# A two-layer transformer kernel: the second attention in row and column parts, five tiles in turns

## The reference

```python
h = _layernorm(x) * (1 + ca) + sa
q = (h @ Wq + bq).reshape(B, S, 16, 32);  kv = (h @ Wkv + bkv).reshape(B, S, 2, 4, 32)   # 4 kv heads
q = apply_rope(q, pos);  k = apply_rope(kv[:, :, 0], pos)
for qs in range(0, S, 128):                       # chunks of 128 queries
    ls = max(16, qs - 127)
    k_c = concat(k[:16], k[ls:qs + 128])           # 16 meta keys, this chunk, the chunk before
    scores = q_c @ k_c.T / sqrt(32)                # masked: causal, and within 128 or meta
    y_c = softmax(scores) @ v_c
x = x + ga * (y @ Wo + bo)
```

## Time and profile before

| | us |
|---|---|
| median of 3 runs | 2404.34 (2399.58 to 2405.88) |
| the profiled execution | 2407.0 |
| its span, first to last instruction | 2405.2 |
| PE busy | 2165.4 (90%) |
| PEld busy | 1492.4 (62%) |
| DVE busy | 1123.3 (47%) |
| ACT busy | 766.4 (32%) |
| POOL busy | 779.6 (32%) |

### The profile page before, as it was taken

How to read it: one execution, slowest core, us unless ns; L and a number is a source line. 1 busy time by engine, 2 the same in 40 slices (tenths; PEclk the granted TensorE clock), 3 DMA queues, 4 the chain that set the end, 5 groups by cost and what they waited for, 6 DMA issues and landing times. The chain is left out here.

```text
span 2405.2 us, 41150 instructions
## 1 busy us (share of the span) xinstructions
PE 2165.4 (90%) x11700; PEld 1492.4 (62%) x11702; DVE 1123.3 (47%) x2783; ACT 766.4 (32%) x1814; POOL 779.6 (32%) x1344
## 2 busy tenths in 40 slices
PE   4799877999999999999916999999994999999998
PEld 2676544555555555555504777777782887878787
DVE  2467575565552222222235676666543454343432
ACT  0233244222222222222202555444552332322322
POOL 0243302223333333333268766677312201101000
PEclk7899888999999999999957999999997999999999
DMA  7555542665565566656443222222001212222220
GB/s 243 183 203 199 218 125 84 195 201 176 183 203 183 191 214 203 203 189 221 136 150 89 72 56 57 72 71 72 2 1 53 70 62 79 62 73 67 72 68 27
DMA packets 122498, 302.21 MB, mean 126 GB/s; under 512 B 24864, under 2 KB 28576, under 8 KB 122272
## 3 DMA queue, kind: packets, MB, share of 16 engines
q1 hardware_dynamic: 73376, 179.04, 22.3%
q0 software_dynamic: 23040, 75.52, 11.1%
q10 hardware_dynamic: 25984, 46.38, 5.2%
HBM read 216.47 MB, written 83.36 MB: 125 GB/s over the span
## 5 line engine op out<-in xcount | busy, mean ns | idle before, releaser
L1167 PE MATMUL bank<-arena 128*128 x1272 | 446.4, 494 | 10.7 <-issue 9.2
L1167 PEld LDWEIGHTS bank<-arena 128*128 128x128 f32 x1272 | 229.8, 191 | 148.5 <-issue 17.9
L1184 PE MATMUL bank<-arena 96*128 x632 | 297.5, 593 | 0.0
L1288 DVE TENSOR_TENSOR arena<-bank,mod 128x512 f32<-128x512 f32 x158 | 109.3, 692 | 214.8 <-PE bank L1184 178.1
L1890 PE MATMUL bank<-x_hi,w_hi 128*128 128x512 f32 x512 | 200.8, 392 | 6.0 <-DVE x_lo L2023 6.0
L1890 PE MATMUL bank<-x_hi,w_lo 128*128 128x512 f32 x512 | 199.4, 389 | 0.0
L1890 PE MATMUL bank<-x_lo,w_hi 128*128 128x512 f32 x512 | 199.2, 389 | 0.0
L1283 DVE TENSOR_TENSOR arena<-arena,bank 128x192 f32<-128x192 f32 x159 | 56.3, 354 | 303.5 <-ACT arena L1205 303.1
L1200 ACT COPY arena<-bank 96x256 f32<-96x256 f32 x158 | 58.2, 368 | 423.2 <-issue 221.2
L1704 DVE TENSOR_REDUCE arena<-bank 128x1 f32<-128x272 f32 x256 | 112.1, 438 | 169.3 <-PE bank L1589 157.8
L1146 POOL DMA_INDIRECT arena<-h_moe,arena x160 | 158.5, 991 | 75.7 <-issue 73.0
(11 more groups left out here) (331 smaller groups left out, 4293.5 us busy)
## 6 DMA issues: line engine op xcount, KB each, us to landing
arena<-in_moe_up SPq DMA_DIRECT2D x64, 768.0 KB, 7.1
y_moe<-arena ACTq DMA_DIRECT2D x158, 256.0 KB, 2.7
y_moe<-mod SPq DMA_DIRECT2D x32, 1024.0 KB
ffn_arena<-in_ffn_up SPq DMA_DIRECT2D x64, 512.0 KB, 3.5
arena<-in_moe_down SPq DMA_DIRECT2D x64, 384.0 KB, 9.4
arena<-in_L_wmod SPq DMA_DIRECT2D x12, 1024.0 KB, 7.0
x_res<-in_L_attn_x SPq DMA_DIRECT2D x1, 4096.0 KB
h_moe<-arena SPq DMA_DIRECT2D x16, 256.0 KB, 6.7
```

The source lines that it names most:

```text
L1167: mm = nc.tensor.matmul(psum[2 + b][:, 0:2 * FI], xgT[:, b, k], up_ring[:, bass.ds((e % RING) * UPW + k * 2 * FI, 2 * FI)], start=(k == 0) ...
L1184: mm = nc.tensor.matmul(psum[6 + b][:], hiddenT[:, b, n], down_ring[:, bass.ds((e % RING) * DOWNW + n * C, C)], start=(n == 0), stop=(n == 1))
L1288: nc.vector.tensor_tensor(y[:, b], psum[6 + b][:], mod[:, 0, 5], ALU.mult).then_inc(y_out, 1)
```

## The change

`schedule` now unrolls 22 turns (m = -4 to 17). A turn works on up to seven tiles: `g` = m+4 (gather), `y` = m+3 (add the experts, statistics), `p` = m+2, `f` = m+1, `s` = m (scores, maxima, exponentials), `a` = m-1 (transposes of the probabilities, values), `w` = m-2 (division, output projection). Heads are handled four at a time (`c` = 0 to 3).

- Scores: four matmuls, each with the 32 rows of one head, into banks 0 to 3. `kT` has no zeros. The mask matmul is gone.
- VectorE adds the mask, negates and takes the minimum in one pass of 272 columns per head (L1690), which writes the negated masked scores to SBUF; a subtraction prepares the meta columns of four heads (L1694).
- ScalarE takes the exponentials in SBUF, 256 columns per head, and once per tile those of all meta columns.
- The probabilities are transposed one tile later, eight transposes for four heads into banks 4 and 5, and copied 512 columns at a time.
- Values: `v` (32 columns) is stationary and 512 columns of transposed probabilities of four heads stream; head group `c` writes partitions 32c to 32c+31 of bank 4. The same with a matrix of ones into bank 5 gives the sums. The meta keys are added by 16 matmuls of 128 columns into each. The result is already transposed: L1647 and L1750 have nothing that answers to them.
- The division is a reciprocal of 128x512 sums and a multiply of 128x512, at the start of VectorE's next turn.
- GpSimd gathers in groups of 3, 2 and 3 (before: eight in a row), the first tile's ahead of its memsets, and reads the positions directly. The values' copies to `v` are gone: VectorE writes them into a ring of five tiles.
- Several buffers lie in `mod[:, 0]` and `down_scale`; `wo` is loaded in four pieces.

```diff
-                    turn(*[tile(t + n) for n in stages])
+                for m in range(-4, NT + 2):
+                    turn(g=tile(m + 4), y=tile(m + 3), p=tile(m + 2), f=tile(m + 1), s=tile(m), a=tile(m - 1), w=tile(m - 2))
...
-                            nc.tensor.matmul(bank, ident_b[:], mask1[:, kind], start=True, stop=False)
-                            nc.tensor.matmul(bank, qT[:, b, n // HP], kT[:, n // HP, n % HP], start=False, stop=True).then_inc(s_mm, 1)
+                def scores(t, c):
+                    if c == 0:
+                        pe.wait_ge(q_in, t + 1)
+                        pe.wait_ge(k_in, t + 1)
+                    pe.wait_ge(mx_done, NHEAD * t + HP * c)
+                    for r in range(HP):
+                        q = slice(HD * r, HD * r + HD)
+                        nc.tensor.matmul(psum[r][:, 0:KEYS1], qT[q, t % 2, c], kT[q, c], start=True, stop=True).then_inc(s_mm, 1)
...
-                            nc.tensor.matmul(out, probT[:, one % 4, 0:P], v[:, 0, c], start=False, stop=False)
+                def turn_probs(t, c):
+                    pe.wait_ge(exp_done, NHEAD * t + HP * c + HP)
+                    if c == 0 and t:
+                        pe.wait_ge(o_out, t)
+                    pe.wait_ge(pT_out, copies_before(t, c))
+                    for k in chunks(t):
+                        for r in range(HP):
+                            at = META + P * k
+                            mm = nc.tensor.transpose(psum[4 + k][:, r * P:(r + 1) * P], slot(t, c)[:, r, at:at + P], ident[:])
...
+                        pe.wait_ge(pT_out, copies_before(a + 1, 0))
+                        pe.wait_ge(pM_out, a + 1)
+                        for bank, local, meta in ((b_o, lambda k, c: v[:, keys_of(a, k) % VRING, c], lambda r, c: v_meta[:, c // 2, r, c % 2]),
+                                                  (b_sum, lambda k, c: ones_f, lambda r, c: meta_sum[:, r, c % 2])):
+                            for k in chunks(a):
+                                for c in range(NKV1):
+                                    nc.tensor.matmul(bank[HD * c:HD * c + HD], local(k, c), probT[:, k, c].rearrange("p r n -> p (r n)"),
+                                                     start=(k == 0), stop=False)
+                            for r in range(HP):
+                                for c in range(NKV1):
+                                    mm = nc.tensor.matmul(bank[HD * c:HD * c + HD, r * P:(r + 1) * P], meta(r, c), metaT[:, c // 2],
+                                                          start=False, stop=(r == HP - 1))
+                                    if r == HP - 1:
+                                        mm.then_inc(o_mm, 1)
...
-                            nc.vector.tensor_reduce(nmx[:, b, n:n + 1], psum[n % 4][:, 0:KEYS1], AX.X, ALU.max,
-                                                    negate=True).then_inc(mx_done, 1)
+                        nc.vector.tensor_tensor_reduce(slot(t, c)[:, r], psum[r][:, 0:KEYS1], mask1[:, kind], -1.0, 3e38, ALU.add, ALU.min,
+                                                       accum_out=nmx[:, t % 2, n:n + 1]).then_inc(mx_done, 1)
+                    dve.wait_ge(mx_done, NHEAD * t + HP * c + HP)
+                    heads = slice(HP * c, HP * c + HP)
+                    nc.vector.tensor_tensor(prob_meta[:, t % 2, heads], nmx[:, t % 2, heads].unsqueeze(2).to_broadcast([P, HP, META]),
+                                            slot(t, c)[:, :, 0:META], ALU.subtract).then_inc(meta_sub, 1)
...
-                    st.did(nc.vector.reciprocal(rs.unsqueeze(2), ob[:, :, HD:V1]))
+                def turn(g, y, p, f, s, a, w):
+                    if w is not None:
+                        dve.wait_ge(o_mm, 2 * NKV1 * (w + 1))
+                        if w:
+                            dve.wait_ge(wo_mm, w)
+                        st.did(nc.vector.reciprocal(osum, b_sum[:]))
+                        st.settle()
+                        nc.vector.tensor_tensor(oT.rearrange("p r n -> p (r n)"), b_o[:], osum, ALU.mult).then_inc(o_out, 1)
+                    if p is not None:
+                        dve.wait_ge(rstd, p + 1)
+                        dve.wait_ge(stats, p + 1)
+                        if p:
+                            dve.wait_ge(hT_mm, p)
+                        nc.vector.tensor_scalar(h, x_res[:, p], st1[:, 6:7], r1[:, 1:2], ALU.subtract, ALU.mult).then_inc(xhat, 1)
...
+                        some = slot(t, c)[:, r, META:KEYS1]
+                        nc.scalar.activation(some, some, ACT.Exp, bias=nmx[:, t % 2, n:n + 1], scale=-1.0).then_inc(exp_done, 1)
...
+                def gather(t, js):
+
+                    if t:
+                        pool.wait_ge(y_sum, TOPK * (t - 1) + js[-1] + 1)
+                    absorb()
+                    for j in js:
+                        nc.gpsimd.indirect_dma_start(out=yg[:, j], out_offset=None, in_=y_moe,
+                                                     in_offset=bass.IndirectOffsetOnAxis(ap=pos_u[:, t, j:j + 1], axis=0)).then_inc(y_in[j], 16)
...
```

More of the change, by code:

```diff
@@ L1368, in adaln_two_layers @@
-            N_DMA = 8
-            def schedule(eng, turn, steps=None, per=0):
-                stages = (4, 3, 2, 1, 0, -1)
-                def tile(t):
-                    return (t, t % 2, t // 2) if 0 <= t < NT else None
-                for t in range(-4, 4):
-                    turn(*[tile(t + n) for n in stages])
-                turns = (NT - 8) // 2
-                with eng.Fori(0, turns) as i:
-                    if steps:
-                        steps.loop(i, per)
-                    for t in (4, 5):
-                        turn(*[(i * 2 + (t + n), (t + n) % 2, i + (t + n) // 2) for n in stages])
-                if steps:
-                    steps.end(turns)
-                for t in range(NT - 4, NT + 1):
-                    turn(*[tile(t + n) for n in stages])
@@ L1528, in _ @@
-                schedule(pool, turn, st, POOL_B)
+                        pool.wait_ge(xhat, w + 1)
+                        nc.gpsimd.tensor_tensor(x_res[:, w], x_res[:, w], bo, ALU.add).then_inc(x_pre, 1)
+                    if g:
+                        gather(g, range(0, 3))
+                    if p is not None:
+                        pool.wait_ge(rope_in[p % 2], 16 * (p // 2 + 1))
+                        pool.wait_ge(q_rows, p + 1)
+                        if p:
+                            pool.wait_ge(roped, p)
+                        rotate(p, slice(0, NHEAD), 0, NHEAD).then_inc(roped_q, 1)
@@ L1530, in _ @@
+                    if g:
+                        gather(g, range(3, 5))
+                    if p is not None:
+                        pool.wait_ge(kv_rows, p + 1)
+                        rotate(p, slice(NHEAD, NQK), 2, NKV1).then_inc(roped, 1)
+                    if g:
+                        gather(g, range(5, TOPK))
+                schedule(turn)
             @block.scalar
@@ new lines, in meta_values @@
+                def meta_values():
+                    head = meta_head.rearrange("p (c r) -> p r c", c=2).unsqueeze(3).to_broadcast([P, HP, 2, HD])
+                    st.did(nc.vector.tensor_copy(meta_sum[:], head))
+                    dve.wait_ge(meta_mm, 1)
+                    for n in range(2):
+                        rows = b_sum[:, n * 2 * HD:(n + 1) * 2 * HD].rearrange("p (c d) -> p c d", c=2)
+                        st.did(nc.vector.tensor_tensor(v_meta[:, n], rows.unsqueeze(1).to_broadcast([P, HP, 2, HD]), head, ALU.mult))
+                    st.settle()
+                    dve.sem_inc(v_meta_done, 1)
@@ L1789, in adaln_two_layers @@
+                schedule(turn)
+                dve.wait_ge(x_out, NT)
         with ExitStack() as ph, nc.Block() as block:
```

593 lines of the change are left out of this document (257 added, 336 removed).

## The result

The changed kernel takes **2419.52 us** (median of 5 runs, 2415.98 to 2421.85), the kernel before 2404.34: ratio 1.0059 (95% interval 1.0039 to 1.0078). It is slower by 0.6%; I had forecast 2396 and faster. The profiled execution took 2415.98 (span 2412.9), 9 us more than that of before. The phase's first VectorE instruction starts at 1207.99 (1214.25 before), its last addition ends at 1820.85 (1814.6): 612.9 us instead of 600.4.

The account below looks back on a forecast made before the run. TensorE's work was taken as the bound: dense run 21.8, head 7.9, slow clock 2.3 and waits 0.6 made a 32.6 us period against 33.0; with start and end, 8 us less, 2396 us (own range 2370 to 2430, overall 2345 to 2460).

Parts of the forecast that it names:

- 24 to 26 now: Start of the phase: a turn costs GpSimd's chain with its wait for the q projection, 24 to 26 us, 25.7 before.
- values 5.7: TensorE's dense run: values, sums and meta matmuls together take 5.7 us a turn.
- Side by side: TensorE's small matmul parts run in parallel on the array, at a factor of 3.7 between bounds 1 and 4.
- Rival (3): Value matmuls: column parts do not run side by side under 128 rows; 2475 at factor 2, 2620 serial; chance 0.2.
- (4): Rival: row parts drain TensorE's array at nine switches, 0.5 us each, 2 us a turn, 2425; within the forecast's 0.5 chance.
- Reciprocal: VectorE's division at the head of a turn: the 128x512 reciprocal takes 3.0 us, bounds 0.7 and 4.2.
- Rival (1): VectorE's reciprocal runs at one element a cycle, 0.7 us: 37 us less, 2359; chance 0.2.
- Head: Start of a turn: chain of reciprocal, multiply, `h`, GpSimd's two passes and hand-overs takes 7.9 us, TensorE nearly idle.
- Clock: TensorE's granted clock falls in each turn's idle head, so the first 4.5 us of dense work lose 2.3 us.
- Rival (2): TensorE's clock stays high or comes back at once: 2.3 us x 16 turns, 2359; chance 0.1.
- the first `x_out` at 1361: End of the start: the first tile's finishing addition comes at 1361, against 1353.6 before, with one more turn in the pipeline.
- TensorE's own work sets the period: Kernel before: TensorE, busy 31.5 us of a 33.0 us stretch, bounds the tile period.

Follow-up runs that it names:

- recip_copy: Changed kernel with the reciprocal of 128x512 sums replaced by a copy of the same size, so the output is not divided: 2353.65 us, ratio 0.978.
- warm: Changed kernel with twelve extra sets of the q transposes on TensorE in the head of a turn, to keep it busy: 2389.93 us, ratio 0.9934.
- pool_one: Changed kernel without GpSimd's multiplication of the normalised row `h` by its scale: 2382.97 us, ratio 0.9906.
- pe_shift23: Changed kernel with 23 extra identity transposes on TensorE at the start of the phase, while it waits anyway: 2390.4 us, ratio 0.994.
- pe_shift: Changed kernel with 64 extra identity transposes on TensorE at the start of the phase, while it waits anyway: 2413.62 us, ratio 1.004.
- before_nomask: Kernel before without the mask's matmul of each score bank, so scores are not masked: 2394.62 us, ratio 0.9953.
- pe_shift_inc: pe_shift with one semaphore increment of 4 per bank in the value section in place of four of 1: 2412.78 us, ratio 1.0032.
- h_first_q: Changed kernel with VectorE's normalisation ahead of the division and TensorE's query projection ahead of the first probability transposes: 2357.25 us, ratio 0.9797.
- best1: h_first_q with the weight multiplies and meta values also moved behind expert additions 5 to 7 of their turn: 2358.10 us, ratio 0.9806.
- best1_inc: best1 with one semaphore increment of 4 per bank in the value section in place of four of 1: 2358.62 us, ratio 0.9787.
- all_parts: h_first_q with one increment of 4 per value bank, and GpSimd's inverse root ahead of the last three gathers: 2372.18 us, ratio 0.9862.
- weights_late: Changed kernel with VectorE's output-weight multiplies and meta values moved behind the expert additions of their turn: 2394.23 us, ratio 0.9956.
- after_again: The changed kernel itself, unedited, run again: 2415.53 us, ratio 1.0052.

## Why the prediction was wrong, by its own steps

Its sum put the phase's last addition at 592 us from the start. Measured: 612.9. Of the 21 us between them, 16 lie ahead of the first `x_out` and 7 in the ten steady intervals; the last five are 2 shorter. Two steps failed: the length of the start's turns ("24 to 26 now") and "values 5.7".

- **Side by side: right.** Sixteen 512-column records in 1.75 us are 109 ns each against 430 for one alone at before's rate of 3.44 us for eight, or 3.9 side by side (I took 3.7). V without the stall is 5.32 us; I had 5.7. Rival (3) is out. So is (4): a score burst takes 0.67 us from its start to that of the next work, for the 0.74 of my sum. (In (3)'s price at a factor of 2, the scores' 6 us should have been 19: three bursts a turn, not one.)
- **Reciprocal: right, a little small.** 3.36 us for 3.0. Rival (1), 0.7 us, was priced at 37 us for the whole kernel, and recip_copy measured 37 by the medians. That is partly luck: 2.3 a turn was near the steady turns' 2.4, but the last five gave 20 where it has 12, and time outside the phase took some back.
- **Head: right.** 7.4 us from burst to `h` transposes for 7.9: the reciprocal 0.36 more, GpSimd's two passes 2.5 in place of 3.3. (VectorE's passes with the mask start every 0.36 us, below my bounds of 0.44 and 0.63.)
- **Clock: mechanism right, price wrong in kind.** It falls each turn (0.87 in place of 1.00) and A pays 2.0 us for it, of 2.3; but warm shows that taking it away gives nearly nothing back. Rival (2) would not have been worth 37 us either.
- **"24 to 26 now" and the first `x_out` at 1361: wrong.** That is 147 us from the start; it took 162.7. The first `h` came 5.6 us sooner than before (28.7 us after the start for 34.3), not 10, and the four turns from it were 28.3, 30.2, 25.2 and 30.0, 114 us for my 100. I had priced GpSimd's chain with one wait, for the q projection. The trace has GpSimd wait for VectorE's third addition, 6.58 us in the second turn, and VectorE for GpSimd's root, 7.46 us:

```profile
1277.15 0.19 POOL L1422 TENSOR_TENSOR arena<-neg_half 128x1 f32<-128x1 f32 x1 [6.58 <-DVE x_res L1701]
```

So the turn looks like a loop through VectorE, GpSimd, TensorE (granted clock 0.62 and 0.61 in the first two) and back. pool_one shows that GpSimd's pass is on it (7 to 10 us off the start for one pass). Neither of my two later reasons, the weights' multiplies and the root's place, was borne out, and the other links were not taken out one by one. Some 2 to 3 us of it are the stall's: the fourth turn takes 27.6 in pe_shift23.

- **"5.7 us" for the values: right without the stall, 6.9 with it.** The ten steady intervals had been put at 326 us; they took 333.2, and 313.5 in pe_shift23. So the steady turn was in truth 1.2 us cheaper than forecast, which pays for the start: pe_shift23, the same work, took 2390.4 us, within 6 of the forecast 2396, and is faster than before by 0.6%. That nearness is luck, 12 us too few in the start against 12 too many in the steady turns. The stall, 23 us by pe_shift and pe_shift23, turned the sign; the start's 16 us alone would have brought the phase back to 597 against 600.4, too near to tell from none.
- **"TensorE's own work sets the period" of before: right by a third.** before_nomask got 0.6 of 1.9 us. The forecast for the new kernel did not rest on it alone.

What stays open: what the stall is. The traces say where it stands. Eight of the eighteen executions profiled after the change have it (the changed kernel twice, pe_shift, pe_shift_inc, h_first_q, best1, best1_inc, all_parts), and then in each of the first eleven value sections; the other ten executions have it in none. In the last five sections, behind GpSimd's last gather, nothing is late in any of the eighteen. Each late section has the issues of GpSimd's last three gathers in or beside it, and in the changed kernel the increments that TensorE owes come 0.3 to 0.4 us after GpSimd's root has ended. But the same gathers at the same places pass without it in weights_late and pe_shift23, so they are at most one of two conditions. The runs exclude a chance execution (after_again) and the number of increments (pe_shift_inc). The clock in it was 1.00. Fetches of instructions, which the trace shows near each V on queue q8, come 0.3 to 6 us after its start, or outside it, in both kinds of kernel. Whether where instructions lie or how turns fall decides it was not separated: 23 extra transposes shift both. No run takes the gathers out of the value section.

## What to carry to other kernels

A reorder that gives an engine less work pays only if what stands in line afterwards is shorter: TensorE's 5.5 us less a turn went into a head of 7.4 us, 5 of which hung on VectorE's order of two independent blocks; swapping them was worth 31 us beside a build without the stall, 60 beside the changed kernel. Before believing that a difference of under 1% comes from a change, compare the same section between harmless variants of the program: here 41 spare transposes moved the time by 23 us. And an engine at 95% busy can be waiting in line: take a piece of its work away before calling it the bound.

## What the hardware showed unexpectedly

- Column parts of 32 under all 128 rows, f32, 512 columns, ran 3.9 side by side.
- A VectorE reciprocal takes 3358 ns on 128x512 from PSUM, the copy of the same 691 ns: 5.2 ns more for each element. Over the 157 ns that the prediction takes as fixed it is 6.3 ns an element, against 4.9 and 5 at 8 and 2 elements.
- The minimum with the mask added is two instructions, 434 and 82 ns; in a burst of four, such a pair starts every 0.36 us, less than the length of one. The plain reductions before (438 ns) never stood in a burst, so no run shows what they would do in one.
- Beside GpSimd's 128x512 passes, VectorE's 128x64 subtraction took 1.29 us (0.23 alone, 479 ns in the mean of 64), and its copy of 128x512 1.50 (0.43 alone).
- In some builds and not in others, the increments of TensorE's value matmuls came 1 to 3 us late around GpSimd's gather issues: TensorE stood still up to 1.0 us in one piece, or VectorE waited with TensorE's work long done.
